# Three neighbouring blocks of x turned on VectorE instead of two, and the frequency work moved within the head's step

## The chip, the cores and the metric

One core of one Trainium2 chip. The metric is the device time of one execution in microseconds (us). The kernel before takes 593.33 us (median of three runs, 591.96 to 594.21).

## The reference, cut to what matters

x has the shape (128, 64, 1024): batch B, head H, position L. For each head a long convolution with a kernel K made from 64 complex exponentials is applied to the masked x, D times the masked x is added, and the result is masked again. Then a top-1 router over 8 experts with rank-16 factors is applied along L, and x is added:

```python
K = 2.0 * einsum('hn,hnl->hl', Cs, exp(P)).real       # P = dtA * arange(L)
y = irfft(rfft(u * mask) * rfft(K))[..., :L] + u * mask * D
y = y * mask
logits = einsum('bsd,ed->bse', y, route_w)             # top 1 of 8
out = x + einsum('bser,eor->bso', onehot_top * einsum('bsd,erd->bser', y, A), Bw)
```

Everything is float32. The kernel writes a float32 factor as a high part of float32r type and a rest, and makes three products (high by high, high by low, low by high).

## The kernel before, in words

The 64 heads are worked through in 64 steps (`run_steps`); in one step each engine works on several heads, `head(d)` being the head d places ahead of step i. The orders on the engines are written out by hand in the five `step` functions, and the engines meet only through counting semaphores (`need`).

The 1024 positions of a head are eight blocks of 128. Even blocks (j = 0) and odd blocks (j = 1) are kept apart: `Xhi` and `Xlo` are [128, 2, 512], so that column group (j, c) is block 2c + j. For one head:

- SyncE loads x of a head to `xt` (batch on the partitions), and `load_blocks` loads some blocks a second time as `xblk`, in 32x32 pieces (8 transfers of 16 KB a head). It writes 3 rows of the convolution kernel to DRAM (`write_kernel`, L409) and reads them back skewed as a Toeplitz matrix `Traw` (`skew_kernel`, L417).
- TensorE turns blocks of `xt` into PSUM (`turn_x`, L1276, six of the eight from head 4 on), brings the block states (`bring`, L1302, sum `psS`), projects the masked result of the head before with the router and the A factors (`project`, L1288, 16 products), makes the inputs (`inputs`, L1319), the products within a block (`within`), those from the states (`from_states`, both at L1262), turns the gated row (`turn_wh`, L1355) and makes the output product (`up`, L1366 to L1371).
- ScalarE copies the turned blocks to `Xhi` (L757), to `xeven` (L769), rounds the state (`s_hi`, L792), the matrices (L744, L750, L700) and `whi` (L797), stores the output (`store`, L774), and copies the first state (`first_state`, L787). `store` stands right before `first_state` of the next step.
- VectorE carries the state over the blocks (`carry`, L1097 and L1101), picks the expert (`largest` to `gated`, L1063 to L1085), makes `Xlo` of the odd blocks (L1043), turns small 32x32 pieces (`turn_k`, L1108; `turn_blocks`, L1050), makes rests (L1114, L1120), masks (`cut`, L1127) and adds x (`add`, L1136).
- GpSimd makes the rests `Slo` (L609), `Xlo` (L595, L602), `Tlo` (L586), `Glo` (L579) and the tables `Wg`, `both`, `Grev` (L573, L553, L565).

Every fourth step a group of four heads (a "part") gets its frequency tables: `angle_steps` on GpSimd (three operations, L534), then `whole_turns`, `high_fraction`, `low_fraction`, `clamp` on VectorE (L1012 to L1035), a sine on ScalarE, `weigh` on GpSimd (three operations, L545) and `mirror` on ScalarE (L693). Before, for steps with i a multiple of 4, GpSimd runs `angle_steps` and `weigh` in the same step, ahead of `g_table` and `s_lo`. On VectorE `whole_turns` and `high_fraction` run in steps with i = 2 modulo 4, `low_fraction` and `clamp` in those with i = 3 modulo 4, both right behind `carry`.

Of the kernel before, what the change touches and what calls it, by code (L numbers as in the profile page):

```python
# [16 lines left out]
F32 = mybir.dt.float32  # L17
F32R = mybir.dt.float32r
I32 = mybir.dt.int32
ALU = mybir.AluOpType  # L20
# [8 lines left out]
def conv_ffn_kernel(nc, x, lens, log_dt, Cw, log_A_real, A_imag, D, route_w, Aw, Bw, out):  # L29
# [11 lines left out]
    G32 = 32  # L41
    G4 = P // G32
    assert B == P and 2 * N == P and ER == P and HALF == 512 and H % 8 == 0

    ctx = ExitStack()
    with ctx:
# [83 lines left out]
        xeven = sb("xeven", [P, HALF])  # L130
        xblk = [sb(f"xblk{s}", [P, 2, G4, G32]) for s in range(4)]
        xlast = [sb(f"xlast{s}", [P, 2, P]) for s in range(2)]
        step_h = [sb(f"step_h{s}", [P, 2, FIRST, G16]) for s in range(2)]
# [130 lines left out]
        blk_in = [sem(f"blk_in{s}") for s in range(4)]  # L264
        xlast_done = sem("xlast_done")
        xhi_last = sem("xhi_last")
        xlo_last = sem("xlo_last")
        s_mm = sem("s_mm")
# [63 lines left out]

        def turned(h):

            return NE - 1 if in_blocks(h) else NE

# [44 lines left out]
        def _(sp):  # L381
# [11 lines left out]

            def load_blocks(h):

                need(sp, xlast_done, blocks_before(h) - 3)
                for j in range(2):
                    for g in range(G4):
                        sp.dma_start(xblk[h.s4][g * G32:(g + 1) * G32, j, :, :],
                                     bass.AP(x.tensor, h.n * L + NS * Q + j * P + g * G32,  # L400
                                             [[H * L, G32], [G32 * H * L, G4], [1, G32]])
                                     ).then_inc(blk_in[h.s4], 16)
# [31 lines left out]
            def step(head):  # L434
                if head(2).there:
                    load_x(head(2))
                if in_blocks(head(3)):
                    load_blocks(head(3))
                if head(2).there:
                    write_kernel(head(2))  # L440
                    skew_kernel(head(2))

# [22 lines left out]
            for s in range(4):  # L465
                sp.wait_ge(blk_in[s], 16 * 2 * G4 * ((H - BLOCK_HEADS) // 4))
            for s in range(2):
# [6 lines left out]
        def _(pool):  # L474
# [115 lines left out]
            def x_lo(h):  # L590

                need(pool, xeven_done, h.n)
                need(pool, y_mm, (h.n - 1) * 2)
                w = turned(h) * P
                pool.tensor_tensor(Xlo[h.s2][:, 0, 0:w], xeven[:, 0:w], Xhi[h.s2][:, 0, 0:w].bitcast(F32),  # L595
                                   ALU.subtract).then_inc(xlo_even, 1)

            def x_lo_last(h):

                need(pool, xhi_last, blocks_before(h) + 1)  # L600
                need(pool, y_mm, (h.n - 1) * 2)
                pool.tensor_tensor(Xlo[h.s2][:, :, NS * P:NE * P], xlast[h.s2][:, :, :],  # L602
                                   Xhi[h.s2][:, :, NS * P:NE * P].bitcast(F32), ALU.subtract).then_inc(xlo_last, 1)

# [7 lines left out]
            def step(head):  # L612
                if head(2).there and not with_matrix(head(2)):
                    w_table(head(2))
                if part_at(head(8)):
                    angle_steps(part_at(head(8)))
                if part_at(head(4)):
                    weigh(part_at(head(4)))
                if head(3).there and not is_head(head(0), 1):
                    g_table(head(3))  # L620
                if head(0).there:
                    s_lo(head(0))
                if head(1).there:
                    x_lo(head(1))
                if head(1).there:
                    t_lo(head(1))
                if is_head(head(0), 1):
                    g_table(head(3))
                    g_lo(head(2))
                if head(3).there:  # L630
                    g_lo(head(3))
                if in_blocks(head(1)):
                    x_lo_last(head(1))

# [22 lines left out]
            g_lo(first[2])  # L657
            angle_steps(parts[2])
            run_steps(step)
# [3 lines left out]
        def _(act):  # L663
# [89 lines left out]
            def x_hi(h, j):  # L753
                need(act, xt_done[j], h.n + 1)
                need(act, y_mm, (h.n - 1) * 2)
                w = turned(h) * P
                act.activation(Xhi[h.s2][:, j, 0:w], psX[j][:, 0:w], ACT.Copy).then_inc(xhi_done, 1)  # L757

            def x_hi_last(h):

                need(act, xlast_done, blocks_before(h) + 1)
                need(act, y_mm, (h.n - 1) * 2)
                act.activation(Xhi[h.s2][:, :, NS * P:NE * P], xlast[h.s2][:, :, :], ACT.Copy).then_inc(xhi_last, 1)

            def x_even(h):

                need(act, xlo_even, h.n)
                w = turned(h) * P
                act.activation(xeven[:, 0:w], psX[0][:, 0:w], ACT.Copy).then_inc(xeven_done, 1)  # L769

# [28 lines left out]
            def step(head):  # L799
# [27 lines left out]
                if is_head(head(0), 2):  # L827
                    act.activation(warm[:, :], quarter[:, :], ACT.Sin)
                if head(0).there:
                    w_hi(head(-1))  # L830
                if in_blocks(head(1)):
                    x_hi_last(head(1))
                if is_head(head(0), 1):
# [86 lines left out]
        def _(dve):  # L920
# [117 lines left out]
            def x_lo(h):  # L1038

                need(dve, xhi_done, h.n * 2 + 2)  # L1040
                need(dve, y_mm, (h.n - 1) * 2)
                w = turned(h) * P
                dve.tensor_tensor(Xlo[h.s2][:, 1, 0:w], psX[1][:, 0:w], Xhi[h.s2][:, 1, 0:w].bitcast(F32),  # L1043
                                  ALU.subtract).then_inc(xlo_odd, 1)

            def turn_blocks(h):

                need(dve, blk_in[h.s4], (blocks_before(h) // 4 + 1) * 16 * 2 * G4)
                need(dve, xlo_last, blocks_before(h) - 1)
                dve.transpose(xlast[h.s2][:, :, :].rearrange("p j b -> p (j b)"),  # L1050
                              xblk[h.s4][:, :, :, :].rearrange("p j g i -> p (j g i)")).then_inc(xlast_done, 1)

# [202 lines left out]
        def _(pe):  # L1255
# [11 lines left out]
            def turn_x(h, j):  # L1267
# [25 lines left out]
            def bring(h):  # L1293
# [203 lines left out]
```

## Time and profile before

| | before |
|---|---|
| median of three runs | 593.33 us (591.96 to 594.21) |
| the profiled execution | 591.81 us |
| its span | 590.0 us |
| TensorE busy | 562.4 us (95%) |
| VectorE busy | 494.2 us (84%) |
| GpSimd busy | 452.1 us (77%) |
| ScalarE busy | 380.7 us (65%) |
| granted TensorE clock, mean | 0.997 of full |
| traffic | 85.61 MB, mean 145 GB/s |

The span is the stretch of the records of the profiled execution; its own time is 1.81 us more. The busy time of an engine leaves out the issuing of transfers: SyncE's queue, which does nothing else, has no share in the table, and its issues are seen in the timeline alone. Engine names in the rows: PE is TensorE, PEld its weight load, DVE is VectorE, ACT is ScalarE, POOL is GpSimd, SPq and ACTq are transfers issued by SyncE and ScalarE.

### The profile page before, as it was taken

The page shows a single profiled execution, that of the slowest core. Times are in us where ns is not written, and L with a number is a line of the kernel's source. Part 1 is how long each engine was busy: PE and PEld are TensorE (multiplying, and loading weights), DVE is VectorE, ACT ScalarE, POOL GpSimd, SP SyncE. Part 2 cuts the span into 40 slices and gives each one's busy share as a digit, 9 for nine tenths or more (in the row PEclk, how much of TensorE's full clock was granted, in tenths as well). Part 3 has the DMA queues.
Part 4 walks back from the last instruction along what each step waited for, and adds up shares of the span by engine and source line. Part 5 has one row for each costly group of instructions (what it writes and reads, how often), then busy time and mean ns, then how long its engine had stood idle before and what let it go on. Part 6 is the DMA issues. An engine that isn't in the chain of part 4 may idle for free.

```text
span 590.0 us, 14019 instructions
## 1 busy us (share of the span) xinstructions
PE 562.4 (95%) x3400; PEld 501.8 (85%) x3400; DVE 494.2 (84%) x1408; ACT 380.7 (65%) x1245; POOL 452.1 (77%) x629
## 2 busy tenths in 40 slices
PE   4799999999999999999999999999999999999996
PEld 4688898988888898898988889899888889889985
DVE  7878888888889888888888888888888888888885
ACT  4777766666676666667667676666767666676630
POOL 5877888778787887878788788877878787787640
PEclk9999999999999999999999999999999999999999
DMA  7135545545645654654554564564565565466522
GB/s 153 51 71 167 153 129 167 175 110 166 177 114 160 176 137 139 175 154 125 170 166 116 169 172 118 159 178 130 146 174 124 149 177 149 129 172 177 135 91 101
DMA packets 107313, 85.61 MB, mean 145 GB/s; under 512 B 81944, under 2 KB 90586, under 8 KB 107234
## 3 DMA queue, kind: packets, MB, share of 16 engines
q1 hardware_dynamic: 97634, 51.19, 37.5%
q10 hardware_dynamic: 9600, 33.53, 14.2%
q8 instruction: 30, 0.49, 0.3%
q14 instruction: 49, 0.40, 0.2%
HBM read 51.02 MB, written 33.65 MB: 144 GB/s over the span
## 4 chain that ended last, share of the span: by engine, by line
PE 61%; DVE 19%; issue 10%; POOL 3%; ACT 2%; ACTq 2%; DVEq 0%; POOLq 0%
PE psYo L1262 13%; PE psZ L1288 12%; PE psYe L1262 10%; PE psS L1262 7%; DVE psS L1097 6%; PE psO L1366 4%; PE psO L1368 4%; PE psO L1371 4%; DVE ost L1136 3%; PE psXe L1276 2%; PE psXo L1276 2%; PE psZ L1355 2%; DVE Sf L1101 2%; ACTq L774 1%; PE psO L1319 1%
## 5 line engine op out<-in xcount | busy, mean ns | idle before, releaser
L1097 DVE SCALAR_TENSOR_TENSOR psS<-Sf,tab,psS 64x128 f32<-64x128 f32 x256 | 91.9, 359 | 59.3 <-ACT Sf L787 52.8
L1288 PE MATMUL psZ<-Wt,Y 128*128 128x136 f32 x1024 | 129.2, 279 | 0.0
L1288 PEld LDWEIGHTS psZ<-Wt,Y 128*128 128x128 f32 x1024 | 123.3, 190 | 0.1
L609 POOL TENSOR_TENSOR Slo<-Sf,Shi 128x384 fp32r<-128x384 f32 x64 | 64.8, 1013 | 72.1 <-ACT Shi L792 72.1
L1136 DVE TENSOR_TENSOR ost<-psO,xt 128x512 f32<-128x512 f32 x127 | 84.6, 683 | 0.8 <-PE psO L1371 0.7
L792 ACT ACTIVATE Shi<-Sf 128x384 fp32r<-128x384 f32 x64 | 33.6, 525 | 76.3 <-DVE Sf L1101 76.3
L553 POOL TENSOR_TENSOR both<-coarse,fine 128x512 f32<-128x512 f32 x64 | 67.7, 1058 | 1.3 <-ACT fine L693 1.2
L595 POOL TENSOR_TENSOR Xlo<-xeven,Xhi 128x384 fp32r<-128x384 f32 (+1 forms) x63 | 64.8, 1029 | 0.0
L717 ACT ACTIVATE cross<-Grev,tabm 64x256 f32<-64x256 f32 x118 | 59.7, 506 | 2.6
L573 POOL TENSOR_TENSOR Wg<-same,cross 128x256 f32<-128x256 f32 x59 | 43.1, 730 | 21.4 <-issue 18.7
L579 POOL TENSOR_TENSOR Glo<-Grev,Ghi 128x256 fp32r<-128x256 f32 x64 | 47.2, 737 | 15.7 <-ACT Ghi L700 15.4
L1127 DVE TENSOR_TENSOR Y<-psYe,mask 128x512 f32<-128x512 f32 x64 | 43.7, 683 | 9.6 <-PE psYe L1262 9.6
L1366 PE MATMUL psO<-Bw_hi,whi 128*128 128x512 f32 x128 | 50.7, 396 | 0.4 <-ACT whi L797 0.4
L1262 PE MATMUL psYo<-Xhi,Thi 128*128 128x512 f32 x128 | 50.7, 396 | 0.0
L565 POOL TENSOR_TENSOR Grev<-both 128x256 f32<-128x256 f32 x64 | 46.8, 731 | 5.0
L1262 PE MATMUL psYo<-Xlo,Thi 128*128 128x512 f32 x128 | 50.6, 395 | 0.0
L1262 PE MATMUL psYo<-Xhi,Tlo 128*128 128x512 f32 x128 | 50.5, 395 | 0.0
L1368 PE MATMUL psO<-Bw_lo,whi 128*128 128x512 f32 x128 | 50.4, 394 | 0.0
L1371 PE MATMUL psO<-Bw_hi,wlo 128*128 128x512 f32 x128 | 50.2, 392 | 0.0
L586 POOL TENSOR_TENSOR Tlo<-Traw,Thi 128x256 fp32r<-128x256 f32 x64 | 47.2, 738 | 3.8 <-ACT Thi L750 3.8
L787 ACT ACTIVATE Sf<-psS 128x128 f32<-128x128 f32 x64 | 17.7, 277 | 47.9 <-PE psS L1262 45.3
L1101 DVE SCALAR_TENSOR_TENSOR Sf<-Sf,tab,psS 128x128 f32<-128x128 f32 x128 | 44.5, 348 | 4.5
(220 smaller groups left out, 1590.9 us busy)
## 6 DMA issues: line engine op xcount, KB each, us to landing
xt<-in_x_dram SPq DMA_DIRECT2D x64, 512.0 KB, 4.8
out_dram<-ost ACTq DMA_DIRECT2D x62, 512.0 KB, 5.1
Traw<-kdram SPq DMA_DIRECT2D x64, 128.0 KB, 2.9
xblk<-in_x_dram SPq DMA_DIRECT2D x480, 16.0 KB, 3.1
kdram<-krow SPq DMA_DIRECT2D x59, 1.5 KB
A_nat<-in_L_ffn_A_dram ACTq DMA_DIRECT2D x1, 512.0 KB, 4.1
B_nat<-in_L_ffn_Bw_dram SPq DMA_DIRECT2D x8, 64.0 KB, 3.0
out_dram<-ost SPq DMA_DIRECT2D x2, 256.0 KB, 2.5
```

What stands on the lines that cost most here:

```text
L553: pool.tensor_tensor(both[:, :, :, :], coarse[:, :, h.n, :].rearrange("p t (a b) -> p t a b", b=1).to_broadcast(wide), fine[:, :, h.n, :]. ...
L595: pool.tensor_tensor(Xlo[h.s2][:, 0, 0:w], xeven[:, 0:w], Xhi[h.s2][:, 0, 0:w].bitcast(F32), ALU.subtract).then_inc(xlo_even, 1)
L609: pool.tensor_tensor(Slo[h.s2][:, :], Sf[h.s2][:, :], Shi[h.s2][:, :].bitcast(F32), ALU.subtract).then_inc(slo_done, 1)
L717: act.activation(cross[to, :], Grev[h.s2][fr, :], ACT.Copy, scale=tabm[fr, MB, h.n:h.n + 1]).then_inc(crossed, 1)
L1097: dve.scalar_tensor_tensor(psS[to, new], Sf[h.s2][fr, old], tab2[fr, BR, h.n:h.n + 1], psS[to, new], ALU.mult, ALU.add).then_inc(brought_d ...
L1101: dve.scalar_tensor_tensor(Sf[h.s2][:, new], Sf[h.s2][:, old], col(tab2[:, LR, :], h), psS[:, new], ALU.mult, ALU.add).then_inc(s_carried, 1)
L1136: dve.tensor_tensor(ost[h.s2][:, half], psO[j][:, :], xt[h.s4][:, half], ALU.add).then_inc(added, 1)
L1262: mm = pe.matmul(dst, a, b, start=first and i == 0, stop=last and i == n - 1, skip_group_check=True)
L1288: last = pe.matmul(psZ[:, 0:NW], Y[:, j, c, :], Wt[:, 2 * c + j, :], start=(j == 0 and c == 0), stop=(j == 1 and c == NE - 1), skip_group_ ...
L1366: pe.matmul(psO[j][:, :], whi[h.s2][:, :], Bw_hi[:, half], start=True, stop=False, skip_group_check=True)
L1368: pe.matmul(psO[j][:, :], whi[h.s2][:, :], Bw_lo[:, half], start=False, stop=False, skip_group_check=True)
L1371: pe.matmul(psO[j][:, :], wlo[h.s2][:, :], Bw_hi[:, half], start=False, stop=True, skip_group_check=True).then_inc(up_mm, 1)
```

## The change

From head 4 on, the blocks that go the second way (loaded in 32x32 pieces and turned on VectorE) are three, column groups (0, 2), (0, 3) and (1, 0), which lie side by side in `Xhi` and `Xlo`. Before they were two, (0, 3) and (1, 3). TensorE turns (0, 0), (0, 1) and (1, 1) to (1, 3). SyncE issues 12 transfers of 16 KB a head, eight ahead of `write_kernel` and four between it and `skew_kernel`. Since `bring` needs the column groups 0 to 2 of both halves, it now waits for the copies of the turned blocks; before, `within` did. `turn_blocks` stands ahead of `x_lo` on VectorE, `x_hi_turn` ahead of `w_hi` on ScalarE, `x_lo_turn` ahead of `t_lo` on GpSimd. `angle_steps` runs one step later, behind `g_table`, and the VectorE work of a part stands at the end of the step, behind `add`.

```diff
+    BLOCK_AT, BLOCKS = 2, 3
-        xblk = [sb(f"xblk{s}", [P, 2, G4, G32]) for s in range(4)]
-        xlast = [sb(f"xlast{s}", [P, 2, P]) for s in range(2)]
+        xblk = [sb(f"xblk{s}", [P, BLOCKS, G4, G32]) for s in range(4)]
+        xturn = [sb(f"xturn{s}", [P, BLOCKS * P]) for s in range(2)]
+        def by_pe(h, j):
+
+            if not in_blocks(h):
+                return range(0, NE)
+            return range(0, BLOCK_AT) if j == 0 else range(BLOCK_AT + BLOCKS - NE, NE)
+
+        def pe_cols(h, j):
+
+            return slice(by_pe(h, j).start * P, by_pe(h, j).stop * P)
+
+        def block_cols(t):
+
+            return t[:, :, :].rearrange("p j w -> p (j w)")[:, BLOCK_AT * P:(BLOCK_AT + BLOCKS) * P]
...
SyncE, step
                 if in_blocks(head(3)):
-                    load_blocks(head(3))
+                    load_blocks(head(3), range(0, BLOCKS - 1))
                 if head(2).there:
                     write_kernel(head(2))
+                if in_blocks(head(3)):
+                    load_blocks(head(3), range(BLOCKS - 1, BLOCKS))
+                if head(2).there:
                     skew_kernel(head(2))
...
GpSimd, step
-                if part_at(head(8)):
-                    angle_steps(part_at(head(8)))
+                if head(3).there and not is_head(head(0), 1):
+                    g_table(head(3))
+                if part_at(head(7)) and not is_head(head(0), 1):
+                    angle_steps(part_at(head(7)))
                 if part_at(head(4)):
                     weigh(part_at(head(4)))
-                if head(3).there and not is_head(head(0), 1):
-                    g_table(head(3))
                 if head(0).there:
                     s_lo(head(0))
                 if head(1).there:
                     x_lo(head(1))
+                if in_blocks(head(1)):
+                    x_lo_turn(head(1))
                 if head(1).there:
                     t_lo(head(1))
                 if is_head(head(0), 1):
+                    angle_steps(part_at(head(7)))
                     g_table(head(3))
                     g_lo(head(2))
                 if head(3).there:
                     g_lo(head(3))
-                if in_blocks(head(1)):
-                    x_lo_last(head(1))
...
-            angle_steps(parts[2])
             run_steps(step)
...
ScalarE, step
+                if in_blocks(head(1)):
+                    x_hi_turn(head(1))
                 if head(0).there:
                     w_hi(head(-1))
-                if in_blocks(head(1)):
-                    x_hi_last(head(1))
...
VectorE, step
                     carry(head(0))
-                if part_at(head(6)):
-                    whole_turns(part_at(head(6)))
-                    high_fraction(part_at(head(6)))
-                if part_at(head(5)):
-                    low_fraction(part_at(head(5)))
-                    clamp(part_at(head(5)))
...
                     gated(head(-1))
+                if in_blocks(head(1)):
+                    turn_blocks(head(1))
                 if head(1).there:
                     x_lo(head(1))
                 if head(2).there:
                     turn_k(head(2))
                     b_lo(head(2))
-                if in_blocks(head(1)):
-                    turn_blocks(head(1))
...
                         add(head(-1), 1)
+                if part_at(head(7)):
+                    whole_turns(part_at(head(7)))
+                    high_fraction(part_at(head(7)))
+                if part_at(head(6)):
+                    low_fraction(part_at(head(6)))
+                    clamp(part_at(head(6)))
...
+            x_lo(first[1])
             carry(first[0])
-            x_lo(first[1])
...
TensorE
-                for c in range(turned(h)):
+                for c in by_pe(h, j):
...
+                if in_blocks(h):                    # in bring
+                    need(pe, xhi_turn, blocks_before(h) + 1)
+                    need(pe, xlo_turn, blocks_before(h) + 1)
...
-                if in_blocks(h):                    # in within
-                    need(pe, xhi_last, blocks_before(h) + 1)
-                    need(pe, xlo_last, blocks_before(h) + 1)
```

## Rows read from the trace of the kernel before

**Rows 1.** Timeline of VectorE: start, duration, engine, line; `carry` and one step's parts.

```profile
70.84 0.75 DVE L1097 SCALAR_TENSOR_TENSOR psS<-Sf,tab,psS 64x128 f32<-64x128 f32 x2 [0.83 <-ACT Sf L787]
...
271.35 0.75 DVE L1097 SCALAR_TENSOR_TENSOR psS<-Sf,tab,psS 64x128 f32<-64x128 f32 x2 [0.83 <-ACT Sf L787]
...
280.40 0.75 DVE L1097 SCALAR_TENSOR_TENSOR psS<-Sf,tab,psS 64x128 f32<-64x128 f32 x2 [0.83 <-ACT Sf L787]
...
288.84 0.75 DVE L1097 SCALAR_TENSOR_TENSOR psS<-Sf,tab,psS 64x128 f32<-64x128 f32 x2 [0.83 <-ACT Sf L787]
...
291.06 0.28 DVE L1012 TENSOR_SCALAR whole<-step_t,quarter 128x128 f32<-128x128 f32 x1
...
291.59 0.16 DVE L1063 TENSOR_REDUCE top<-psZ 128x1 f32<-128x8 f32 x1
...
292.57 0.29 DVE L1085 TENSOR_TENSOR wh<-psZ,gate 128x128 f32<-128x128 f32 x1
...
294.10 0.25 DVE L1120 TENSOR_TENSOR wlo<-psZ,whi 128x128 fp32r<-128x128 f32 x1
...
295.46 1.27 DVE L1136 TENSOR_TENSOR ost<-psO,xt 128x512 f32<-128x512 f32 x2
297.57 0.75 DVE L1097 SCALAR_TENSOR_TENSOR psS<-Sf,tab,psS 64x128 f32<-64x128 f32 x2 [0.83 <-ACT Sf L787]
...
524.69 0.75 DVE L1097 SCALAR_TENSOR_TENSOR psS<-Sf,tab,psS 64x128 f32<-64x128 f32 x2 [0.89 <-ACT Sf L787]
```

**Rows 2.** Timeline of ScalarE: the end of a mirroring step, and a store.

```profile
276.51 0.40 ACT L700 ACTIVATE Ghi<-Grev 128x256 fp32r<-128x256 f32 x1
...
278.99 0.51 ACT L719 ACTIVATE same<-Grev,tabm 128x256 f32<-128x256 f32 x1
...
288.04 0.37 ACTq L774 DMA_DIRECT2D out_dram<-ost  x1
288.53 0.28 ACT L787 ACTIVATE Sf<-psS 128x128 f32<-128x128 f32 x1 [0.73 <-PE psS L1262]
```

**Rows 3.** Timeline of TensorE: a stall ahead of the products from the states, and one whole step.

```profile
276.17 0.41 PE L1262 MATMUL psYe<-Shi,Ghi 128*128 128x384 f32 x1 [0.69 <-issue]
...
288.15 0.49 PE L1276 MATMUL psXe<-ident,xt 128*128 128x128 f32 x3
288.48 0.49 PE L1276 MATMUL psXo<-ident,xt 128*128 128x128 f32 x3
...
292.98 0.27 PE L1355 MATMUL psZ<-ident,wh 128*128 128x128 f32 x1
...
296.59 0.49 PE L1276 MATMUL psXe<-ident,xt 128*128 128x128 f32 x3
```

**Rows 4.** Timeline of GpSimd: a step with both kinds of part work, one without.

```profile
271.33 0.40 POOL L534 TENSOR_TENSOR step_t<-tab,grid 128x128 f32<-128x128 f32 x1
...
275.06 1.00 POOL L609 TENSOR_TENSOR Slo<-Sf,Shi 128x384 fp32r<-128x384 f32 x1
...
283.34 1.02 POOL L609 TENSOR_TENSOR Slo<-Sf,Shi 128x384 fp32r<-128x384 f32 x1 [1.15 <-ACT Shi L792]
```

**Rows 5.** Groups by line and shape: busy us, mean ns, idle before.

```profile
L792 ACT ACTIVATE Shi<-Sf 128x384 fp32r<-128x384 f32 x64 | 33.6, 525 | 76.3 <-DVE Sf L1101 76.3
...
L1050 DVE STREAM_TRANSPOSE xlast<-xblk 128x256 f32<-128x256 f32 x60 | 25.4, 424 | 0.0
...
L1108 DVE STREAM_TRANSPOSE krow<-kcol 128x96 f32<-128x96 f32 x64 | 17.2, 268 | 1.8 <-ACT kcol L725 1.8
```

**Rows 6.** Timeline of SyncE's queue: two bursts of block loads, and two single issues.

```profile
288.43 4.30 SPq L399 DMA_DIRECT2D xblk<-in_x_dram  x8
...
293.54 0.54 SPq L409 DMA_DIRECT2D kdram<-krow  x1
295.22 0.34 SPq L417 DMA_DIRECT2D Traw<-kdram  x1
...
463.34 5.33 SPq L399 DMA_DIRECT2D xblk<-in_x_dram  x8
```

More of the change, by code:

```diff
@@ L264, in conv_ffn_kernel @@
         blk_in = [sem(f"blk_in{s}") for s in range(4)]
-        xlast_done = sem("xlast_done")
-        xhi_last = sem("xhi_last")
-        xlo_last = sem("xlo_last")
+        xturn_done = sem("xturn_done")
+        xhi_turn = sem("xhi_turn")
+        xlo_turn = sem("xlo_turn")
         s_mm = sem("s_mm")
@@ L331, in blocks_before @@
             return max(h.n - BLOCK_HEADS, 0)
-        def turned(h):
-            return NE - 1 if in_blocks(h) else NE
+        def by_pe(h, j):
[6 more added lines that the diff above has]
+            return t[:, :, :].rearrange("p j w -> p (j w)")[:, BLOCK_AT * P:(BLOCK_AT + BLOCKS) * P]
         def weighed_before(h):
@@ L392, in load_x, with load_blocks @@
                 sp.dma_start(xt[h.s4][:, :], head_rows(x, h)).then_inc(x_in[h.s4], 16)
-            def load_blocks(h):
-                need(sp, xlast_done, blocks_before(h) - 3)
-                for j in range(2):
+            def load_blocks(h, blocks):
+                need(sp, xturn_done, blocks_before(h) - 3)
+                for b in blocks:
+                    j, c = divmod(BLOCK_AT + b, NE)
                     for g in range(G4):
-                        sp.dma_start(xblk[h.s4][g * G32:(g + 1) * G32, j, :, :],
-                                     bass.AP(x.tensor, h.n * L + NS * Q + j * P + g * G32,
+                        sp.dma_start(xblk[h.s4][g * G32:(g + 1) * G32, b, :, :],
+                                     bass.AP(x.tensor, h.n * L + c * Q + j * P + g * G32,
                                              [[H * L, G32], [G32 * H * L, G4], [1, G32]])
@@ L465, in _ @@
             for s in range(4):
-                sp.wait_ge(blk_in[s], 16 * 2 * G4 * ((H - BLOCK_HEADS) // 4))
+                sp.wait_ge(blk_in[s], 16 * BLOCKS * G4 * ((H - BLOCK_HEADS) // 4))
             for s in range(2):
@@ L593, in x_lo, with x_lo_turn @@
                 need(pool, y_mm, (h.n - 1) * 2)
-                w = turned(h) * P
-                pool.tensor_tensor(Xlo[h.s2][:, 0, 0:w], xeven[:, 0:w], Xhi[h.s2][:, 0, 0:w].bitcast(F32),
+                cols = pe_cols(h, 0)
+                pool.tensor_tensor(Xlo[h.s2][:, 0, cols], xeven[:, cols], Xhi[h.s2][:, 0, cols].bitcast(F32),
                                    ALU.subtract).then_inc(xlo_even, 1)
-            def x_lo_last(h):
-                need(pool, xhi_last, blocks_before(h) + 1)
+            def x_lo_turn(h):
+                need(pool, xhi_turn, blocks_before(h) + 1)
                 need(pool, y_mm, (h.n - 1) * 2)
-                pool.tensor_tensor(Xlo[h.s2][:, :, NS * P:NE * P], xlast[h.s2][:, :, :],
-                                   Xhi[h.s2][:, :, NS * P:NE * P].bitcast(F32), ALU.subtract).then_inc(xlo_last, 1)
+                pool.tensor_tensor(block_cols(Xlo[h.s2]), xturn[h.s2][:, :], block_cols(Xhi[h.s2]).bitcast(F32),
+                                   ALU.subtract).then_inc(xlo_turn, 1)
             def s_lo(h):
@@ L755, in x_hi, with x_hi_turn @@
                 need(act, y_mm, (h.n - 1) * 2)
[L756 to L761, printed above, removed]
+                cols = pe_cols(h, j)
+                act.activation(Xhi[h.s2][:, j, cols], psX[j][:, cols], ACT.Copy).then_inc(xhi_done, 1)
+            def x_hi_turn(h):
+                need(act, xturn_done, blocks_before(h) + 1)
                 need(act, y_mm, (h.n - 1) * 2)
-                act.activation(Xhi[h.s2][:, :, NS * P:NE * P], xlast[h.s2][:, :, :], ACT.Copy).then_inc(xhi_last, 1)
+                act.activation(block_cols(Xhi[h.s2]), xturn[h.s2][:, :], ACT.Copy).then_inc(xhi_turn, 1)
             def x_even(h):
                 need(act, xlo_even, h.n)
-                w = turned(h) * P
-                act.activation(xeven[:, 0:w], psX[0][:, 0:w], ACT.Copy).then_inc(xeven_done, 1)
+                cols = pe_cols(h, 0)
+                act.activation(xeven[:, cols], psX[0][:, cols], ACT.Copy).then_inc(xeven_done, 1)
             def store(h):
@@ L1041, in x_lo @@
                 need(dve, y_mm, (h.n - 1) * 2)
-                w = turned(h) * P
-                dve.tensor_tensor(Xlo[h.s2][:, 1, 0:w], psX[1][:, 0:w], Xhi[h.s2][:, 1, 0:w].bitcast(F32),
+                cols = pe_cols(h, 1)
+                dve.tensor_tensor(Xlo[h.s2][:, 1, cols], psX[1][:, cols], Xhi[h.s2][:, 1, cols].bitcast(F32),
                                   ALU.subtract).then_inc(xlo_odd, 1)
             def turn_blocks(h):
[L1048 to L1051, printed above, removed]
+                need(dve, blk_in[h.s4], (blocks_before(h) // 4 + 1) * 16 * BLOCKS * G4)
+                need(dve, xlo_turn, blocks_before(h) - 1)
+                dve.transpose(xturn[h.s2][:, :],
+                              xblk[h.s4][:, :, :, :].rearrange("p j g i -> p (j g i)")).then_inc(xturn_done, 1)
             def x_lo_even(h):
```

## The prediction

> **What bounds the kernel now.** The page has TensorE at 95%, so the first question is what its other 5% are and what else is near it. I read the page, then the chain of waits (it changes several times between TensorE and VectorE, which says that two loops are near each other), then the timeline of each engine over some steps, and SyncE's queue, which no busy share shows.
>
> `carry` opens VectorE's part of each step. Its starts repeat in a cycle of four: steps of 9.05 us (28, i = 0 modulo 4), 8.44 (29), 8.73 (30) and as much for the fourth [rows 1]. From step 5 (70.84) to step 57 (524.69) that is 453.85 us for 13 cycles, 34.91 each [rows 1]. Three things make up the cycle:
>
> - TensorE's own work. In step 29 it goes from one turning of x to the next in 8.44 us (288.15 to 296.59) and has no idle time in it [rows 3]. This floor holds wherever nothing else is longer.
> - VectorE with ScalarE's store. From `carry` at 288.84 to the end of `add` at 296.73 VectorE needs 7.89; then come the issue of the store, 0.37, the first state `Sf`, 0.28, and the handing over, 0.84 in all up to the next `carry` at 297.57 [rows 1, 2]. That is 8.73, and part work of 0.53 is in it (291.06 to 291.59) [rows 1]. Without part work the loop is 8.20, so TensorE's 8.44 wins; with it VectorE wins. So the two steps with part work cost 0.29 each above TensorE's.
> - GpSimd in step 28. It runs the three angle operations and the weighing ahead of `g_table`, and `Slo` starts at 275.06, 3.73 behind the first of them, with no wait [rows 4]. TensorE stands idle 0.69 ahead of the products from the states [rows 3]. In step 29, without part work, `Slo` waited 1.15 for ScalarE, so GpSimd has that much room [rows 4].
>
> **The change part by part.**
>
> *TensorE.* Three turned blocks take 0.33 (288.15 to 288.48), one 0.11 [rows 3]. The floor falls from 8.44 to 8.33. The Trainium skill, "VectorE: DVE Perf Modes", section "The three transpose paths", gives 390 ns for a 128x128 transpose on TensorE, of bf16; the trace does not agree for blocks turned back to back. With that figure 60 heads would free 23 us of TensorE and not the 6.6 that 0.11 gives, but the rest of this sum does not use it.
>
> *VectorE.* The transposition grows from 256 to 384 columns. It takes 424 ns at 256 and 268 at 96 [rows 5], so 0.98 ns a column, 0.125 us more; in proportion to the whole duration it would be 0.21, and 0 if hidden. I take 0.125, the row's own slope. The part work moves behind `add`, where VectorE stands idle for 0.83 in each step until `Sf` [rows 1]; 0.53 fits there, in different steps (i = 1 and 2 modulo 4). If it didn't fit, its old price of 0.29 a step would be back. VectorE's loop becomes 8.20 + 0.125 = 8.33 in all steps, as long as TensorE's. That two loops are equal leaves no slack for small delays.
>
> *GpSimd.* Its two Xlo operations swap widths (384 and 256 before, 256 and 384 after), nothing in sum. The weighing stays in step i = 0, the angles (three of at most 0.40, so 1.2) move to i = 1. The room is 1.15 [rows 4]: at most 0.05 over, which I take as nothing. TensorE's stall goes. The wait of `bring` for the turned blocks ends well ahead: `Slo`, `Xlo`, and the new one at about 1.0 each, from 283.34, end near 286.3, and in that step `bring` comes some 1 us before 288.15, near 287.1 [rows 3, 4]. Before `t_lo` and `g_lo` stand 1.0 us of new work; their readers are a step away.
>
> *ScalarE.* The copies swap widths too. But `x_hi_turn` now stands ahead of `w_hi`, and VectorE's `w_lo`, `cut` and `add` queue behind `whi`. `wh` ends at 292.86, 4.02 behind `carry`, 3.49 without part work [rows 1]. The transposition then ends at about 4.04, the copy of 384 columns takes 0.525 [rows 5], `whi` 0.28 as `Sf` of the same shape [rows 2]: ready by 4.75 to 4.85. `w_lo` stands at 5.26 less 0.53 plus 0.125, so 4.86 [rows 1]. The slack is 0.0 to 0.1. Cost between nothing and the full copy less that slack, 0.43 a step; I take nothing, since the estimate says that it just fits. In the steps i = 0 the mirroring follows: from `Ghi` to the end of `same` took 2.99 (276.51 to 279.50) [rows 2]; from 4.7 that ends at 7.7, while the store is due at 8.33 - 0.84 = 7.5. So I give this step 0.15 more.
>
> *SyncE.* Twelve block loads instead of eight. A burst of eight issues takes 4.30 or, at worst, 5.33 [rows 6], so 0.54 to 0.67 each; twelve take 6.45 to 8.00. The write takes 0.54, the read back 0.34, the load of x I take as the latter, with handings over 0.15: 1.37 [rows 6]. The queue's loop is 7.8 to 9.4 against a step of 8.33. Most bursts are near the short one, and the four added issues stand late in the step, when the large transfers of x and of the output have been issued for 5 us and more. I take 8.0, so nothing. The write of the kernel waits for `turn_k`, now 0.48 later (behind a transposition of 0.55 that overlaps), but the wait for its landing is filled by the four loads.
>
> *Start and end.* The angle operations of part 2 leave the preamble for step 1, ahead of `g_table`: between 0 and 1.2, taken as 0.3, because `Slo` in step 1 gets earlier by most of it. Steps 2 to 4 have one stalled step and two with part work, like a cycle without its short step: -1.1.
>
> *The sum.* New cycle: 3 x 8.33 + 8.48 = 33.47 against 34.91, 1.44 less; 13 cycles 18.7. The last six steps, at TensorE's floor, 6 x 0.11 = 0.7. Start -0.3 + 1.1 = 0.8. Together 20.2. The span goes from 590.0 to 569.8, the profiled execution from 591.8 to 571.6, and the median, 1.5 above that execution, from 593.3 to 573.1.
>
> **The rivals.**
>
> 1. *Clean floor.* ScalarE is not late in any step: cycle 33.32, 2 us more gained: 571. It belongs to the forecast.
> 2. *A new wait takes a part back.* For: ScalarE's slack of 0.0 to 0.1 ahead of `w_lo`, and two loops of one length. If `whi` is 0.2 late in 59 steps, 12 us come back: 585. If the angles still make `Slo` late, by the 0.69 of before, about 0.6 a cycle, 8 us: 581. Against: the room of 1.15 on GpSimd. With the whole copy exposed, 0.43 x 59 = 25, there would be no gain: 598.
> 3. *SyncE's queue becomes the loop* (the other side). It decides nothing below 8.33, eats the gain from there, and makes the kernel slower when its loop is above the present mean step, 34.91 / 4 = 8.73, that is at (8.73 - 1.37) / 12 = 0.61 an issue. For: a burst at 0.67 was seen. At 0.64 the loop is 9.05, 0.32 above the present step, times 59: 612. At 0.59, 8.45: 580. Against: the slow bursts are few, and loads run one to two steps ahead of their use, so that only the mean counts. The Trainium skill, "DMA: Bandwidth & Descriptors", section "Bandwidth", holds transfers under 64 KB to be dominated by their descriptors and fits 2.0 us and a small term to each. By that rule alone the four 16 KB loads would be an estimated 8 us of transfer a head, and one after another they would make this rival true. The issues of a burst follow each other at 0.54, so they overlap, and the trace bears the rule out only as to the time of one.
> 4. *The blocks land late for `turn_blocks`*, now 1.5 us earlier in the step: they are loaded two steps ahead, so this is only a consequence of rival 3.
>
> **How the numbers follow.** Forecast with rival 1: 0.62, own range 570 to 578. Rival 2: 0.18, of which 0.02 with no gain and 0.01 slower. Rival 3 with a part of the gain left: 0.08; as large as the gain: 0.03; slower: 0.05. Something unseen that leaves it within 0.5% 0.02, or slower 0.02. A measurement tells about 0.5% from no change. So faster: 0.62 + 0.15 + 0.08 = 0.85, same 0.07, slower 0.08. The range starts at the floor of both loops, 20.2 + 2 + the spread of the median of 1.2 below 593.3, so 569, and takes in rivals 2 and 3 up to 585; that leaves out nearly 2 in 10.
>
> **What would show it.** Steps of `carry` all near 8.33, the one with mirroring 8.5; no idle time of TensorE ahead of the products from the states; part work on VectorE inside the idle time ahead of `carry`; the transposition at 0.55; `Xhi` of the turned blocks ahead of `whi`, and no wait of `wlo` for it. Wrong would be: `wlo` waiting for `whi` in all steps (rival 2), loads of x issued later and later after `add` (rival 3), or a step above 8.6.

## The result

| | before | changed |
|---|---|---|
| median of 20 runs | 593.23 us (591.74 to 595.54) | 596.75 us (594.64 to 603.34) |
| ratio to before | | 1.0064, 95% interval 1.005 to 1.0078 |
| the profiled execution | | 596.18 us, span 594.4 us |
| traffic | 85.61 MB | 89.56 MB |

The forecast was 573.1 us, in a range of 569 to 585. The kernel became 0.64% slower, and the interval leaves out no change: the forecast missed by 24 us and by the sign.

The timeline of VectorE in the changed kernel, `carry` first, then the end of step 29; these lines answer to [rows 1].

```profile
67.63 0.75 DVE L1112 SCALAR_TENSOR_TENSOR psS<-Sf,tab,psS 64x128 f32<-64x128 f32 x2 [0.81 <-ACT Sf L802]
...
271.38 0.75 DVE L1112 SCALAR_TENSOR_TENSOR psS<-Sf,tab,psS 64x128 f32<-64x128 f32 x2 [0.81 <-ACT Sf L802]
...
279.69 0.75 DVE L1112 SCALAR_TENSOR_TENSOR psS<-Sf,tab,psS 64x128 f32<-64x128 f32 x2 [0.81 <-ACT Sf L802]
...
286.21 1.28 DVE L1151 TENSOR_TENSOR ost<-psO,xt 128x512 f32<-128x512 f32 x2
287.41 0.46 DVE L1027 TENSOR_SCALAR whole<-step_t,quarter 128x128 f32<-128x128 f32 x1
287.90 1.05 DVE L1034 SCALAR_TENSOR_TENSOR frac<-whole,step_h 128x128 f32<-128x128 f32 x1
...
526.90 0.75 DVE L1112 SCALAR_TENSOR_TENSOR psS<-Sf,tab,psS 64x128 f32<-64x128 f32 x2 [0.82 <-ACT Sf L802]
```

From step 5 to step 57 it is 459.27 us, 35.33 a cycle where 33.47 was forecast and 34.91 was before. Step 28 is as forecast: 271.38 to 279.69, 8.31 us. So the step without part work that was summed is real. But `carry` of step 30 starts at 288.98: step 29 has 9.29 us. Two things lie in it.

First, the part work. `add` ends at 287.49 and the two operations end at 288.95: 1.46 us for what was to be 0.53, longer than the 0.83 of idle time. GpSimd's timeline in the same stretch of the changed kernel:

```profile
287.04 0.75 POOL L588 TENSOR_TENSOR Wg<-same,cross 128x256 f32<-128x256 f32 x1
287.74 1.06 POOL L568 TENSOR_TENSOR both<-coarse,fine 128x512 f32<-128x512 f32 x1
```

`whole` ends at 287.87, 0.08 after `Wg` (287.79); `frac` ends at 288.95, 0.15 after `both` (288.80). Each ends shortly behind GpSimd's instruction; that it waits for that one is a reading so far, which the runs below test. In [rows 1] `whole` lay at 291.06, 2.22 behind `carry`, in a stretch in which GpSimd of the kernel before did nothing, from 290.47 to 291.78:

```profile
291.78 1.02 POOL L609 TENSOR_TENSOR Slo<-Sf,Shi 128x384 fp32r<-128x384 f32 x1 [1.30 <-ACT Shi L792]
```

The groups of the changed kernel, with mean duration in ns. The first three of the 16 parts are worked on at the start of the kernel, beside other work; in the 13 behind them `frac` takes 1042 to 1047 ns each time. The transposition of 384 columns isn't touched, though it too runs beside GpSimd (283.34 to 283.91, with `Slo` from 282.69 to 283.71); it has one input, as `whole` has, so the number of inputs alone doesn't decide:

```profile
L1065 DVE STREAM_TRANSPOSE xturn<-xblk 128x384 f32<-128x384 f32 x60 | 34.1, 568 | 0.0
...
L1034 DVE SCALAR_TENSOR_TENSOR frac<-whole,step_h 128x128 f32<-128x128 f32 x16 | 15.6, 977 | 0.5
```

Second, SyncE's queue. Its waits in the changed kernel from step 5 to step 57 (67.63 to 526.90), in us in total, times, longest:

```profile
SPq L421 <- DVE krow L1123: 10.7, 21, 0.9
SPq L403 <- DVE ost L1151: 0.4, 2, 0.3
SPq L378 <- DMA kdram<-krow: 0.3, 1, 0.3
```

The load of x waited for `add` only twice, 0.4 us: in nearly every step SyncE came to it late. All waits are 11.4 us, 0.22 in each of the 52 steps. A step lasts 459.27 / 52 = 8.83, so issuing and handing over take 8.61, above the 8.33 that the other loops were to need. A cut of the queue's timeline in the changed kernel:

```profile
303.49 2.96 SPq L411 DMA_DIRECT2D xblk<-in_x_dram  x4
306.56 0.39 SPq L429 DMA_DIRECT2D Traw<-kdram  x1
306.99 0.48 SPq L403 DMA_DIRECT2D xt<-in_x_dram  x1
307.52 4.38 SPq L411 DMA_DIRECT2D xblk<-in_x_dram  x8
311.99 0.54 SPq L421 DMA_DIRECT2D kdram<-krow  x1
312.57 1.86 SPq L411 DMA_DIRECT2D xblk<-in_x_dram  x4
```

Four loads take 1.86 in one step and 2.96 in another; the burst of eight is as before [rows 6]. And what hangs on the queue, in the waits of the engines over the whole run:

```profile
ACT Thi L765 <- DMA Traw<-kdram: 15.7, 23, 1.3
...
DVE wlo L1135 <- ACT whi L812: 11.6, 20, 1.0
```

### The profile page after: what moved, and what is told of

The parts are those of the page before. It is cut to its first block, busy times and chain, and to the rows that moved or that the text cites. A ratio compares the mean times of both kernels' runs of the same rounds, so it can differ in the third digit from the quotient of the medians.

```text
span 594.4 us, 14079 instructions
## 1 busy us (share of the span) xinstructions
PE 567.8 (96%) x3340; PEld 494.6 (83%) x3340; DVE 521.7 (88%) x1408; ACT 367.7 (62%) x1245; POOL 451.0 (76%) x629
## 2 busy tenths in 40 slices
DMA packets 141874, 89.56 MB, mean 151 GB/s; under 512 B 116504, under 2 KB 125146, under 8 KB 141794
## 4 chain that ended last, share of the span: by engine, by line
DVE 30%; SPq 18%; issue 18%; PE 12%; DMA 9%; ACT 5%; POOL 3%; ACTq 1%; DVEq 0%; POOLq 0%
SPq L411 14%; DMA Traw<-kdram 9%; DVE psS L1112 8%; DVE ost L1151 5%; DVE Y L1142 3%; PE psZ L1303 2%; PE psYo L1277 2%; DVE Sf L1116 2%; PE psYe L1277 2%; DVE Xlo L1058 2%; SPq L421 2%; DVE gate L1094 2%; DVE psZ L1083 1%; PE psS L1277 1%; DVE best L1088 1%
## 5 line engine op out<-in xcount | busy, mean ns | idle before, releaser
L1151 DVE TENSOR_TENSOR ost<-psO,xt 128x512 f32<-128x512 f32 x127 | 81.5, 678 | 0.7 <-PE psO L1386 0.7
L617 POOL TENSOR_TENSOR Xlo<-xturn,Xhi 128x384 fp32r<-128x384 f32 x60 | 61.1, 1018 | 13.3 <-ACT Xhi L778 12.1
L1381 PE MATMUL psO<-Bw_hi,whi 128*128 128x512 f32 x128 | 52.7, 412 | 3.7 <-ACT whi L812 3.4
L610 POOL TENSOR_TENSOR Xlo<-xeven,Xhi 128x256 fp32r<-128x256 f32 (+1 forms) x63 | 48.1, 764 | 0.0
```

The costliest lines, as they stand in the source:

```text
L617: pool.tensor_tensor(block_cols(Xlo[h.s2]), xturn[h.s2][:, :], block_cols(Xhi[h.s2]).bitcast(F32), ALU.subtract).then_inc(xlo_turn, 1)
L1151: dve.tensor_tensor(ost[h.s2][:, half], psO[j][:, :], xt[h.s4][:, half], ALU.add).then_inc(added, 1)
L1381: pe.matmul(psO[j][:, :], whi[h.s2][:, :], Bw_hi[:, half], start=True, stop=False, skip_group_check=True)
```

## The experiments

Two theories: *port* (the part work waits for GpSimd) and *queue* (SyncE issues too much). Each ratio is to the kernel before on the same chip, with its 95% interval. L numbers are those of each kernel. Five runs leave something out: where the third block isn't loaded (three runs), and where it is loaded as rows and not in pieces (two), the output is that of other data. The runs in order of the argument:

| run | median us | ratio |
|---|---|---|
| changed, third block not loaded | 585.52 | 0.9866 (0.9839 to 0.9894) |
| changed, part work behind `carry` | 594.24 | 1.0021 (1.0003 to 1.0039) |
| both | 584.52 | 0.9846 (0.9816 to 0.9877) |
| before, part work behind `add` | 602.48 | 1.0157 (1.012 to 1.0193) |
| third not loaded, GpSimd waits | 570.06 | 0.9619 (0.9593 to 0.9645) |
| changed, GpSimd waits | 589.86 | 0.9959 (0.9932 to 0.9986) |
| the same, ten loads then two | 591.89 | 0.9983 (0.9965 to 1.0002) |
| two blocks, GpSimd waits | 573.31 | 0.9672 (0.9648 to 0.9697) |
| third block in one transfer | 570.29 | 0.9622 (0.96 to 0.9644) |
| third block in four, few packets | 588.13 | 0.9928 (0.9903 to 0.9952) |
| four loads from ScalarE | 579.88 | 0.9782 (0.9751 to 0.9813) |
| four from ScalarE ahead of store | 580.75 | 0.9791 (0.9743 to 0.984) |
| ten and two | 573.45 | 0.9675 (0.9648 to 0.9702) |
| before, part work hidden | 581.81 | 0.9822 (0.9794 to 0.985) |
| before, angles moved | 590.28 | 0.995 (0.9931 to 0.9969) |

**The third block not loaded.**

```diff
-                if in_blocks(head(3)):
+                if in_blocks(head(3)) and head(3).n < BLOCK_HEADS + 4:
                     load_blocks(head(3), range(BLOCKS - 1, BLOCKS))
...
```

> The changed kernel, but the third block is loaded only for the first head of each buffer; later heads turn and use what lies there, so SyncE issues 8 block loads a head and the output is that of other data. Two theories. Port: the part work on VectorE (4 operations) runs against GpSimd behind add and costs 1.5 us instead of 0.6 in two steps of four; the loads matter little. Then the two part steps stay near 9.0 and the time falls only to about 590 us. Queue: SyncE's queue with 12 loads is late, so the Toeplitz matrix and what hangs on it are late. Then all steps fall to 8.3 to 8.5 and the time to 573 to 576 us.

585.5 us; the ratio falls from 1.0064 with the loads to 0.9866, by 2.0% or 11.7 us. The port theory alone had 590, the queue theory alone 573 to 576: neither explains the whole.

**The part work back behind `carry`.**

```diff
                     carry(head(0))
+                if part_at(head(6)):
+                    whole_turns(part_at(head(6)))
+                    high_fraction(part_at(head(6)))
+                if part_at(head(5)):
+                    low_fraction(part_at(head(5)))
+                    clamp(part_at(head(5)))
...
-                if part_at(head(7)):
-                    whole_turns(part_at(head(7)))
-                    high_fraction(part_at(head(7)))
-                if part_at(head(6)):
-                    low_fraction(part_at(head(6)))
-                    clamp(part_at(head(6)))
```

> The changed kernel with whole_turns, high_fraction, low_fraction and clamp back behind carry (steps i = 2 and 3 modulo 4), all else changed. Port: GpSimd waits for ScalarE there, the four operations take 0.28, 0.29, 0.35, 0.23 us again, the cycle of four steps is 8.33 + 8.86 + 8.86 + 8.48 = 34.5 us and the time about 586 us. Queue: nothing on SyncE has changed, so the time stays at about 596 us.

594.2: 2.5 us less, not 10. The operations were short again (`frac` 293 ns at the median), but the step stayed long: the queue had as many issues as before the edit.

**Both edits.**

> Both edits at once: third block not loaded after the first heads, and the part work back behind carry. Port alone: as with the part work moved back only, about 586 us. Queue alone: as without the third loads only, about 573 us. If both are real and each covers the other, it is clearly below both single edits, down to 34.5 us a cycle, 585 us or less.

584.5, 1.0 us below the first run, and the intervals overlap. So with the queue out of the way, part work slowed behind `add` costs about as much as part work at full speed behind `carry`: in both places some 0.5 to 0.6 us in each step that has it (steps of 8.86 to 8.96 where the others have 8.33), instead of nothing.

**The kernel before, part work behind `add`.** The same lines moved as in the change, nothing else.

> The kernel before with one edit: the part work on VectorE stands behind add, in steps i = 1 and 2 modulo 4; two blocks, 8 loads, nothing else. Port: the four operations take 0.44, 1.04, 0.48 and 0.96 us as in the changed kernel, the two steps go from 8.44 and 8.73 to about 8.9 and 8.9, the fourth falls to 8.42, and the time is 0 to 5 us above the kernel before. Queue: the operations are hidden in the idle time ahead of carry, and the time falls to about 586 us.

602.5, 1.6% slower, with no third block and no added load. The port theory had the sign, but not the size. The four groups there:

```profile
L1019 DVE SCALAR_TENSOR_TENSOR frac<-whole,step_h 128x128 f32<-128x128 f32 x16 | 15.3, 954 | 0.5
...
L1035 DVE TENSOR_SCALAR fraction<-frac 128x128 f32<-128x128 f32 x16 | 14.6, 913 | 0.5
...
L1027 DVE SCALAR_TENSOR_TENSOR frac<-step_l,quarter,frac 128x128 f32<-128x128 f32 x16 | 12.2, 764 | 0.0
...
L1012 DVE TENSOR_SCALAR whole<-step_t,quarter 128x128 f32<-128x128 f32 x16 | 9.5, 592 | 0.0
```

They sum to 3.2 us a part, and to 2.8 in the changed kernel; `whole` and the low part are the longer ones (592 and 764 ns against 444 and 465), `frac` of the high part isn't. The move alone costs 10 us.

**GpSimd made to wait.** If GpSimd is the cause, it can be kept out of the way: it has idle time later in those two steps.

```diff
GpSimd, step
+                if part_at(head(6)):
+                    need(pool, frac1_done, part_at(head(6)).k + 1)
+                if part_at(head(5)):
+                    need(pool, frac_done, part_at(head(5)).k + 1)
                 if head(2).there and not with_matrix(head(2)):
                     w_table(head(2))
```

Once without the loads of the third block, once with them.

> The third block is not loaded after the first heads (as in the first run, other data there), and GpSimd waits ahead of w_table until VectorE's part work behind add is done, in steps i = 2 and 3 modulo 4; it has idle time later in those steps. Port: the part work takes 0.53 us again and now lies in VectorE's idle time ahead of carry; all steps go to 8.33 to 8.48 us, the cycle to 33.5, the time to 573 to 576 us, which is what was forecast for the change. If something other than GpSimd slows these operations, they stay at 1.5 us and the time at 585 us.

> The changed kernel, all three blocks loaded, with the same wait of GpSimd. Queue: SyncE's loop of 8.45 us or more a step binds, and the late Toeplitz matrix delays whi; the time is 585 to 592 us. If the queue mattered only together with the slow part work, the time is 573 to 577 us.

Without the loads: 570.1 us, 2.5% or 14.6 us under the run without this wait. The groups and the timeline of VectorE and GpSimd in that kernel:

```profile
L1038 DVE SCALAR_TENSOR_TENSOR frac<-whole,step_h 128x128 f32<-128x128 f32 x16 | 5.9, 369 | 0.5
```

```profile
285.96 0.33 DVE L1046 SCALAR_TENSOR_TENSOR frac<-step_l,quarter,frac 128x128 f32<-128x128 f32 x1
286.33 0.23 DVE L1054 TENSOR_SCALAR fraction<-frac 128x128 f32<-128x128 f32 x1
286.87 0.75 DVE L1116 SCALAR_TENSOR_TENSOR psS<-Sf,tab,psS 64x128 f32<-64x128 f32 x2 [0.32 <-ACT Sf L806]
```

```profile
286.63 0.73 POOL L588 TENSOR_TENSOR Wg<-same,cross 128x256 f32<-128x256 f32 x1 [1.06 <-DVE fraction L1054]
```

The mean of 369 ns has the first three parts in it; in the 13 behind them `frac` takes 291 to 293 ns. The part work now takes 0.60 (285.96 to 286.56) and ends 0.3 before `carry`. VectorE's own orders are the same in both runs, so GpSimd's work at that place is the cause. This is the run that has the forecast's conditions, and its time is within 3 us of it. A wait added on one engine freed 14.6 us on another.

With all loads: 589.9, so 20 us hang on four more issues in each step once nothing else is longer. SyncE's waits there from step 5 to step 57, beside the kernel without the loads (second fence):

```profile
SPq L421 <- DVE krow L1127: 2.0, 8, 0.4
SPq L403 <- DVE ost L1155: 1.8, 5, 0.5
SPq L378 <- DMA kdram<-krow: 0.3, 1, 0.3
```

```profile
SPq L378 <- DMA kdram<-krow: 67.2, 51, 2.0
SPq L403 <- DVE ost L1155: 27.4, 44, 0.9
SPq L421 <- DVE krow L1127: 13.3, 33, 0.7
SPq L378 <- POOL Tlo L601: 1.2, 1, 1.2
```

4.1 us against 109. With all loads `carry` goes from 67.29 to 522.09 in these 52 steps, 8.75 each, of which 0.08 is waiting: the queue's loop is 8.67 and sets the step. Without them the step is 8.36 and the loop 6.26.

**Order or length of the queue.** Ten loads ahead of the kernel rows' write and two behind it.

> As the changed kernel with GpSimd's wait, but ten of the twelve loads stand ahead of the write of the kernel rows and two behind it, so that the read back of the Toeplitz matrix is issued about 1 us sooner. If the queue costs by the lateness of that matrix: 3 to 8 us below the run with eight and four. If it costs by the length of its loop alone: the same time.

591.9, no gain. But the edit didn't make the matrix come earlier where it is used: `Thi` waits 29.1 us for it in sum, and 29.0 with eight and four. So the run shows that this order doesn't help, and it doesn't tell the lateness of the matrix from the length of the loop. The next runs shorten the loop.

**Issues or packets.** The third block as one transfer of 128 rows, and as four of 32 rows.

```diff
-                    load_blocks(head(3), range(BLOCKS - 1, BLOCKS))
+                    sp.dma_start(xblk[head(3).s4][:, BLOCKS - 1, :, :].rearrange("p g i -> p (g i)"),
+                                 bass.AP(x.tensor, head(3).n * L + P, [[H * L, P], [1, P]])
+                                 ).then_inc(blk_in[head(3).s4], 16)
...
```

> The changed kernel with GpSimd's wait; the third block is loaded by one transfer of 128 rows of 512 bytes from SyncE instead of four of 32x32 pieces, so it isn't laid out in pieces (the output is that of other data): same bytes, 9 issues instead of 12, 128 packets instead of 512. Issuing as the cause: SyncE's loop falls to about 7.0 us and the time to 571 to 574 us. Bytes as the cause: 585 us or more.

> As the run with the third block in one transfer, but in four transfers of 32 rows of 512 bytes: 12 issues on SyncE, 128 packets (the output is that of other data). If each issue costs SyncE its 0.44 us or more whatever it moves, the loop is as long as with pieces, the time 585 to 590 us. If an issue costs by its packets, the four take about as long as the one, and the time is 570 to 573 us.

One transfer: 570.3, as good as no load, with all bytes moved (89.54 MB). Four transfers of as many packets in sum: 588.1. Both move the same bytes in the same rows, so the number of issues decides. The duration of an issue there, min/median/max in ns, for 128 pieces (first line) and for 32 rows:

```profile
L411 SPq DMA_DIRECT2D xblk<-in_x_dram x480: 312/440/1807, 31.1 to 548.0; - x160
L455 SPq DMA_DIRECT2D xblk<-in_x_dram x240: 333/422/1717, 36.7 to 550.6; - x120
```

A quarter of the packets goes with 18 ns less of 440; the two stand at different places in the queue, so a part of that may be the place.

**Who issues.** All three blocks loaded, part of the issues on ScalarE, and as many fewer on SyncE.

```diff
ScalarE
+            def load_third(h, pieces):
+
+                need(act, xturn_done, blocks_before(h) - 3)
+                for g in pieces:
+                    act.dma_start(xblk[h.s4][g * G32:(g + 1) * G32, BLOCKS - 1, :, :],
...
+                if in_blocks(head(2)) and head(-1).there:
+                    load_third(head(2), (2, 3))        # ahead of store
...
+                if in_blocks(head(3)):
+                    load_third(head(3), (0, 1))        # behind x_even
...
```

> The changed kernel with GpSimd's wait, and the four loads of the third block issued by ScalarE, two behind x_even and two ahead of store; SyncE issues 8. All data is loaded. If SyncE's issuing is the cause, the time falls from 590 us to 572 to 578 us (ScalarE pays up to 0.9 us in the mirroring steps). If the transfer engines are the cause, the same packets still move, and the time stays at 585 to 590 us.

> The changed kernel with GpSimd's wait, eight loads from SyncE and all four others from ScalarE ahead of store, none behind x_even. All data is loaded. The earlier run with two behind x_even had 579.9 us, and there these two took up to 1.4 us against the large transfers. Without them: 573 to 577 us, with up to 1.0 us lost in each mirroring step.

> The changed kernel with GpSimd's wait, ten loads from SyncE and two from ScalarE ahead of store, where ScalarE is idle for 1.3 us in three steps of four. All data is loaded. SyncE's loop falls from 8.6 to about 7.5 us: below the step, so 572 to 578 us. If the loads from ScalarE disturb through the transfers of x and of the output, about 580 us as with four from ScalarE.

579.9 and 580.8 with four, both above their expectation, and 573.5 with two ahead of `store`. The same packets as in the changed kernel move in all three, so the transfer engines aren't the cause of its time. With all four ahead of `store`, ScalarE is idle for 13.2 us ahead of `Sf` in 8 steps, and the profile names no other engine for it:

```profile
ACT Sf L813 <- issue: 13.2, 8, 2.5
```

In six of the eight, one issue on ScalarE took 1.3 to 2.1 us (median 454 ns for a block load, 378 for a store). With two ahead of `store` no issue on ScalarE is over 0.9 us. Why four bring such issues isn't shown.

**Two blocks.** `BLOCKS = 2`, all eight loads ahead of the write, GpSimd's wait, the rest as in the change.

> The changed kernel with two blocks, (0, 2) and (0, 3), 8 loads all ahead of the write of the kernel rows, and the wait of GpSimd. TensorE turns six blocks again, its floor is 8.42 us; VectorE's loop is 8.33 (transposition 0.13 shorter, Xlo 0.13 longer). Both theories: cycle 33.8 us, time 578 to 580 us. If steps of 8.42 don't hold, a loop is missing in both.

573.3 us, 3.3% faster than before, below what was expected, with a mean step of 8.42 as it was taken for TensorE. It and the run with ten and two are equal, and are the fastest kernels here that compute everything. So the third block gives back on TensorE, 0.11 us a step, about what its issues cost, even with two of them on ScalarE.

**The kernel before, with only the frequency work changed.**

> The kernel before with its two blocks and its order of turning, and only: angle_steps a step later behind g_table, the part work of VectorE behind add, and GpSimd's wait for it. Port: all steps at TensorE's floor of 8.42 us, cycle 33.8, time 576 to 579 us. If the moved turning of the blocks is needed as well, it is clearly above the 573 us of the two-block version, 580 us or more.

> The kernel before with one edit: angle_steps a step later and behind g_table. TensorE's stall of 0.7 us in every fourth step goes, the two steps with part work behind carry stay at 8.73: cycle 8.42 + 8.42 + 8.73 + 8.73 = 34.3 us, time 585 us. If the angles in the next step make Slo late there, the stall only moves and the time stays at 592 us.

581.8 and 590.3, both some 3 to 5 us above their expectation. The angles alone give 0.5%, not 1.3%: the stall moves in part to the next step. The steps i = 0 modulo 4 fall from 9.05 to 8.34 and those behind them rise from 8.42 to 8.87 (medians). GpSimd's timeline in that kernel, from the step behind the mirroring one:

```profile
314.61 0.73 POOL L573 TENSOR_TENSOR Wg<-same,cross 128x256 f32<-128x256 f32 x1 [1.20 <-ACT cross L717]
...
317.12 0.40 POOL L534 TENSOR_TENSOR step_t<-tab,grid 128x128 f32<-128x128 f32 x1
...
318.19 1.01 POOL L609 TENSOR_TENSOR Slo<-Sf,Shi 128x384 fp32r<-128x384 f32 x1
```

`w_table` waits 1.20 for ScalarE's `cross`, which comes behind the mirroring, and the angles' 1.07 then push `Slo`. In the two-block version ScalarE turns to `Ghi` 4.65 behind `carry` in the mirroring step, where the kernel before with part work hidden has 5.16, and the whole is 8.5 us faster (573.3 against 581.8); I argue from this that moving the turned blocks forward matters for GpSimd, but no run moved that alone.

## Why the prediction was wrong

**The steps that failed are two: "0.53 fits there, in different steps", and for SyncE "I take 8.0, so nothing".**

1. *VectorE's part work.* The idle time of 0.83 was there, and 0.53 fits in it when nothing else happens (0.60 in the run with GpSimd's wait). But the durations were taken from a place where GpSimd was idle, and the new place is one where it works. They took 1.46 in step 29. The sum had counted on hiding 0.53 in 26 steps, 13.8 us; the run with the wait against the one without gives 14.6. The Trainium skill has this, "SBUF — State Buffer", section "Who interferes with whom": a VectorE instruction that reads two inputs from SBUF, or runs in a two-port mode, contends with GpSimd, and whichever issues second is blocked for the whole of the other's instruction. The trace agrees: both operations began behind GpSimd's and ended 0.08 and 0.15 behind its ends. That remainder is shorter than the whole operation alone (0.28 and 0.29), which no run here explains; nor does one show which of the two kinds `whole` and `fraction` are. The bound "its old price of 0.29 a step would be back" was too low even by the prediction's own loops: 0.29 was what 8.73 stood above TensorE's 8.44, but with TensorE and VectorE both at 8.33 the whole 0.53 counts. The run with both edits has the part work at its old place and costs some 14 us more than the one that hides it, about 0.53 in each of 26 steps.
2. *SyncE's queue.* Rival 3 named it, with 0.16 of the chance, of which 0.05 for slower. The mechanism was seen and the term was mis-sized: 8.0 was taken, and 8.61 is measured in the changed kernel, 8.67 with the part work hidden. What it had missed is that single issues don't keep their time when the queue is full. The load of x had been put at the read back's 0.34; from step 5 to step 57 both now take 0.56 on average (0.35 and 0.34 before), some 0.4 a step together. The issue of the load of x in the changed kernel and (second fence) in the kernel before, min/median/max in ns:

```profile
L403 SPq DMA_DIRECT2D xt<-in_x_dram x64: 346/439/1777, 2.9 to 562.2; - x64
```

```profile
L392 SPq DMA_DIRECT2D xt<-in_x_dram x64: 346/347/588, 2.9 to 557.5; - x64
```

   Not all of this comes from the number of issues: without the third block's loads the load of x still has 0.50 on average, while the read back is at 0.34 again. The rest lies in the block loads and the handing over. "Only the mean counts" held: by rival 3's own reckoning a loop of 8.67 against 8.73 leaves 0.06 x 59, 3.5 us of gain, 590, and 589.9 was measured. In the changed kernel the slow part work came on top. The fit of 2.0 us that rival 3 quotes stands in the Trainium skill, "DMA: Bandwidth & Descriptors", section "Anatomy of one DMA — SWDGE (gpsimd) path", for transfers that GpSimd issues, and not under "Bandwidth"; here SyncE issues them, and what bound was the issuing.
3. *The sum otherwise held.* TensorE's 0.11, the transposition, the two equal loops of 8.33: the run with both faults removed goes from `carry` at 69.60 to `carry` at 504.30 in 52 steps, 8.36 each, and takes 570.1 us against 573.1. The step with the mirroring, given 0.15 more, is no longer than the others: rival 1, worth 2 of these 3 us. The transposition grew by 568 - 424 = 144 ns [rows 5], where 125 was taken.
4. *ScalarE ahead of `w_lo`* (rival 2). `wlo` waited 20 times, 11.6 us in all. Four of these lie in the first and last steps; in the 16 others `Thi` had waited for the Toeplitz matrix in the same step (step 30: `Thi` 0.49, then `wlo` 0.24). Without the third block's loads the four are all that is left. So it was a consequence of rival 3.
5. *GpSimd's room for the angles.* It held in the changed kernel (in step 29 `Slo` starts at 282.69, 0.14 behind the end of `Shi`); in the kernel before, it doesn't. The room of 1.15 was read behind a step that the stall itself had made 9.05 long. There `w_table` began 0.77 ahead of `carry` (279.63 and 280.40); with the stall gone it begins 0.06 ahead (314.61 and 314.67), since it waits for the mirroring, and 0.7 of the room is lost.

How the 26.7 us above the run with the forecast's conditions divide: from 570.1, part work not hidden, to 585.5; the loads, to 596.75, so 15 and 11. In the other order (loads first, to 589.9; part work, to 596.75) the shares are 20 and 7: the two overlap, since a late queue hides part of the late VectorE.

## What to carry to other kernels

A duration belongs to the place where it was measured: before an elementwise operation of VectorE on SBUF tensors is moved into idle time, look at what GpSimd does there, and if it works, the price is up to the rest of its instruction, as it was here. A wait on the engine that has time to spare can cost nothing and give the whole gain back. Count the issues of a DMA queue like the work of an engine, its handing over and slow issues too; the small transfers of this kernel cost by their number and hardly by their packets, and where one engine's queue is full, two issues on another at its idle place did what four didn't. When two loops come out as long as each other, any work put back into one of them costs its full time.

## What was not expected of the hardware

- How much a blocked instruction grows: the last of the four part operations takes 0.23 us alone and 913 ns on average behind `add` in the kernel before, `whole` 0.28 [rows 1] and 592 ns on average.
- A single issue on SyncE spreads from 0.31 to 2.08 us in the changed kernel, with a median of 433 ns for the block loads.
- The landing of the Toeplitz matrix goes from 2.9 us before to 4.5 in the changed kernel and that of x from 4.8 to 5.8 (medians). Only a part of it belongs to the four added issues: without them and with the part work hidden, the matrix lands in 3.7 and x in 5.8. Meanwhile the transfer engines' share in the steps goes only from 0.55 to 0.57:

```profile
67.77:527.04 459.27, 449.68 (x2654) 392.51 (x2654) 411.98 (x1093) 292.23 (x1003) 365.19 (x495) 1.00 0.57 158
```

  (the view by stretches of the changed kernel, steps 5 to 56: length, busy time of TensorE, its weight load, VectorE, ScalarE and GpSimd, granted clock, share of the transfer engines, GB/s; the granted clock of 1.00 is 2.4 GHz).
